# Second dense layer of the last MLP as fp32r in two parts, last y made by ScalarE from z, buffers of the second graph layer dealt out as they fall free

## Chip, core and metric

The kernel runs on one core of one Trainium2 chip. The metric is the device time of one execution in microseconds (us). Tiles are given as partitions x elements. All data are fp32 in memory; the matmuls work either on fp32 directly or on fp32r, a rounded form of the same width.

## Reference

```python
# x, x2: 4096 x 128; adj: 4096 x 4096
def cxin_conv(x, a, eps, W, b):
    ax = a @ x
    h = ax + (1.0 + eps[0]) * ax
    for i in range(3):
        h = relu(h @ W[i].T + b[i])
    return h
out1, out2 = cxin_conv(x, adj, eps1, W1, b1), cxin_conv(x2, adj, eps2, W2, b2)
x = layernorm(x + concatenate((out1, out2), axis=1) @ Wm.T + bm)
A_hat = adj + eye(4096)
d = rsqrt(sum(A_hat, axis=1))
x = layernorm(x + ((d[:, None] * A_hat * d[None, :]) @ x) @ W.T + b)
```

## The kernel before, in words

Everything is kept transposed. The adjacency is read twice, in four quarters of 1024 rows (QW) each: once for graph layer 0 (products with x and x2), once for graph layer 1 (product with y, the normalised x times the degree factor d). A quarter has 32 tiles (JB) of 128 x 1024, loaded in pairs of 1 MB by SP (`load` L371). Each tile is split in two fp32r parts: ScalarE rounds it to a high part (`round_a` L652, the activation at L684), VectorE subtracts to get the low part (`split_a` L838, L851), and TensorE multiplies high by high, high by low and low by high (`products` L465, L506). So a tile costs 12 matmuls of 512 columns in layer 0 and 6 in layer 1. The parts live in rings: four slots in layer 0 (SPLIT), six in layer 1 (SPLIT2); slots 4 and 5 of layer 1 are the tile hhi (high) and alo_extra (low), chosen by `ring_hi` L310 and `ring_lo` L318. A slot may be overwritten when TensorE has finished the tile six (in layer 0, four) back (`used_ahead` L323).

Pairs of layer 0 sit in four places (raw). Layer 1 has eight: raw and raw2; raw2 lies over x2 in memory and its parts fall free one after the other in quarter 3 of layer 0 (`load2` L381). Pair p of layer 1 goes to place p mod 8, first raw 0 to 3, then raw2 0 to 3 (`raw_tile` L266).

The order on each engine is written by hand: every engine runs the same loop over the tiles n of a quarter and does, at steps given by constants (L69 to L103), the extra work of the quarter before. That work (plan 0 for quarters 0 to 2, plan 1 for the last one, which falls in quarter 0 of layer 1) is: ScalarE evacuates the products to h (L698), three dense layers (`dense` L512) each followed by a ReLU (`relu` L701), the merge with Wm (`merge` L528), then the residual and statistics on VectorE (`residual` L884, `statistics` L923, `aggregate` L933), the power on GpSimd (`norm_power` L1156), `shifts` L945, and ScalarE's `normalise` L710, which writes xn. VectorE turns and sums the row sums (`turn_rowsums` L890, `add_turned` L895), SP carries them through memory (L386, L391), VectorE makes the degrees and the factors d (`degrees` L902, `degree_factors` L916). In plan 0 the dense layers are three fp32r passes over hhi and hlo, in plan 1 one fp32 matmul; there they stand behind tiles 1, 2 and 3, the merge behind tile 4.

```python
                    if plan == 0:
                        wait(pe, hlo_ready, q * (LAYERS * M) + (M * l + m + 1))
                        passes = ((whi, hhi), (whi, hlo), (wlo, hhi))
                    else:
                        wait(pe, h_ready, q * (4 * M) + (M * l + m + 1))
                        passes = ((par, h),)
```

y of a quarter is made in three steps: `make_y` L985 (VectorE, xn times d to yt), `round_y` L735 (ScalarE), `split_y` L996 (VectorE). The y of the last quarter is needed by TensorE at tile 24 of quarter 0 of layer 1 (L618). Before a tile of the diagonal is rounded, VectorE adds the identity to its square of 128 (`add_identity` L1015); in quarter 0 of layer 1 these are tiles 0 to 7, each added three steps ahead (AHEAD), so that three fall in the last steps of layer 0 and five in layer 1.

Of the kernel before, what the change touches and what calls it, by code (L numbers as in the profile page):

```python
# [67 lines left out]

PE_DENSE = ({3: 0, 5: 1, 8: 2}, {1: 0, 2: 1, 3: 2})  # L69
PE_MERGE = (10, 4)  # L70
PE_PROJECT = 1
# [4 lines left out]
ACT_EVACUATE = (2, 2)  # L76
ACT_RELU = tuple({k + ahead: l for k, l in plan.items()} for plan, ahead in zip(PE_DENSE, AHEAD_OF_PE))
DVE_RESIDUAL = tuple(k + ahead for k, ahead in zip(PE_MERGE, AHEAD_OF_PE))
STATISTICS = (2, KB)
TB = 32  # L80
GROUPS = P // TB
DVE_AGGREGATE = (DVE_RESIDUAL[0] + 1 + KB // STATISTICS[0], DVE_RESIDUAL[1])
DVE_DEGREES = tuple(k + 1 + plan for plan, k in enumerate(DVE_RESIDUAL))
DVE_FACTORS = (DVE_AGGREGATE[0] + 2, DVE_DEGREES[1] + 3)
DVE_TURN = (5, 4)
DVE_BASE = 10
DVE_BASE_LAST = 20
DVE_SHIFT = tuple(k + 2 for k in DVE_AGGREGATE)
ACT_NORM = (22, 14)
ACT_COPY_AY = 3  # L90
DVE_MAKE_Y = (KB + 4, 2 * KB + 4, 3 * KB + 3, 18)
NORM_BLOCKS = (2, 2)
# [20 lines left out]
SECOND_TILE = [(b, c, k) for c in range(CH) for b in range(2) for k in (0, 2)]  # L113
SECOND_TILE += [(b, c, 1) for c in range(CH) for b in range(2)]
X_AFTER = {1: 1, 3: 2, 6: 3, 12: 4, 20: 5}


def build(nc, a_t, head, early, x12, params, scratch, out):
    with ExitStack() as ctx:
# [22 lines left out]
        xn = sb("xn", [P, QUARTERS, QW])  # L142
        raw = sb("raw", [P, RAW, 2, QW])
        ahi = sb("ahi", [P, SPLIT, QW], F32R)
        alo = sb("alo", [P, SPLIT, QW], F32R)
        h = sb("h", [P, M, CW])
        hhi = sb("hhi", [P, M, CW], F32R)
        rowsum_all = sb("rowsum_all", [P, QW])
        xb = sb("xb", [P, KB, P])
# [23 lines left out]
        degpow = sb("degpow", [P, KB])  # L173
        dall = sb("dall", [P, QUARTERS, KB])

        ps = [ctx.enter_context(nc.psum_tensor(f"ps{i}", [P, CW], F32)) for i in range(M)]
# [49 lines left out]
        d_ready = sem("d_ready")  # L226
        yt_ready = sem("yt_ready")
        yhi_ready = sem("yhi_ready")
        base_ready = sem("base_ready")
# [36 lines left out]
        def raw_tile(layer, n):  # L266

            p = n // 2
            if layer == 0:
                return raw[:, p % RAW, n % 2, :]  # L270
            p %= RAW + RAW2
            return raw[:, p, n % 2, :] if p < RAW else raw2[:, p - RAW, n % 2, :]

        def wait_raw1(eng, q, n):

            s, turn = n // 2 % (RAW + RAW2), n // 2 // (RAW + RAW2)
# [33 lines left out]
        def ring_hi(layer, q, n):  # L310

            i = slot(layer, q, n)
            if i >= SPLIT:
                m = 2 * (i - SPLIT)
                return hhi[:, m:m + 2, :].rearrange("p m w -> p (m w)")
            return ahi[:, i, :]

# [28 lines left out]
        def _(sp):  # L346
# [34 lines left out]
            def load2(g):  # L381

                sp.wait_ge(block_used, (QUARTERS - 1) * JB + (g + 1) * KB)
                load(raw2[:, g], RAW + g).then_inc(raw2_in[g], 16)

# [39 lines left out]
            for s in range(RAW):  # L425
                sp.wait_ge(raw_used, groups * RAW + s + 1 - RAW)
                load(raw[:, s], s).then_inc(raw_in[s], 16)
                if s == 0:
                    load2(2)
            load2(3)  # L430
            turns = groups * RAW // (RAW + RAW2)

            def load1(g, s):

                sp.wait_ge(lo_ready, g * (2 * (RAW + RAW2)) + (QUARTERS * JB + 2 * (s + 1 - RAW - RAW2)))
                dst, landed = (raw[:, s], raw_in[s]) if s < RAW else (raw2[:, s - RAW], raw2_in[s - RAW])
                load(dst, g * (RAW + RAW2) + s).then_inc(landed, 16)

            for s in range(RAW + RAW2):
                load1(1, s)  # L440
                if s == 2:
                    spread_partial(LAST)
                if s == 3:
                    gather_partial(LAST)
            with sp.Fori(2, turns - turns // QUARTERS) as g:
                for s in range(RAW + RAW2):
                    load1(g, s)
            for m in range(PAIRS):

                s, c = m % (RAW + RAW2), m // (PAIRS // CH)  # L450
# [3 lines left out]
                for r, done in enumerate((unit_in[s], landed)):  # L454
                    sp.dma_start(dst[:, r, :].rearrange("p (t w) -> p t w", w=CW),
                                 a_t[pair + r][:, :, c * CW:(c + 1) * CW]).then_inc(done, 16)
# [7 lines left out]
        def _(pe):  # L464
# [179 lines left out]
        def _(act):  # L644
# [7 lines left out]
            def round_a(q, layer, n):  # L652
# [19 lines left out]
                else:  # L672
# [28 lines left out]
            def relu(q, l, plan):  # L701
                for m in range(M):
# [16 lines left out]
            def mlp_step(q, n, plan):  # L719
# [7 lines left out]
                at, size = ACT_NORM[plan], NORM_BLOCKS[plan]  # L727
                if at <= n < at + KB // size:
# [98 lines left out]
        def _(dve):  # L827
# [39 lines left out]

            def split_h(q, l, m):

                wait(dve, hhi_ready, q * (LAYERS * M) + (M * l + m + 1))  # L870
                dve.tensor_tensor(hlo[:, m, :], h[:, m, :], as_f32(hhi[:, m, :]),  # L871
                                  ALU.subtract).then_inc(hlo_ready, 1)
# [78 lines left out]
            def mlp_step(q, n, plan):  # L951
                if plan == 0:
                    if n in (ACT_EVACUATE[0] + 1, ACT_EVACUATE[0] + 2):
                        for m in range(CH):
                            split_h(q, 0, CH * (n - ACT_EVACUATE[0] - 1) + m)
                    if n in ACT_RELU[0] and ACT_RELU[0][n] < LAYERS - 1:
                        for m in range(M):
                            split_h(q, ACT_RELU[0][n] + 1, m)
                if n == DVE_TURN[plan]:
                    turn_rowsums(q)  # L960
                if n == DVE_TURN[plan] + 1:
                    add_turned(q)
# [94 lines left out]
            def layer0_quarter(q, before):  # L1057
                for n in range(JB):
# [8 lines left out]
                    if q is QUARTERS - 1:  # L1067
# [82 lines left out]
        def _(pool):  # L1150
# [22 lines left out]
            with pool.Fori(0, QUARTERS - 1) as q:  # L1173
                degree_power(q)
                norm_power(q + 1)
            norm_power(QUARTERS)
            degree_power(QUARTERS - 1)
            for q in range(QUARTERS - 1):
# [46 lines left out]
```

## Time and profile before

| | before |
|---|---|
| times of three runs | 593.35, 595.50, 595.93 us, median 595.5 |
| the profiled execution | 593.42 us, span 591.6 |
| granted TensorE clock in the profile | 1.000 |
| TensorE busy | 584.4 us, 99% |
| VectorE busy | 542.0 us, 92% |
| ScalarE busy | 372.3 us, 63% |
| GpSimd busy | 28.2 us, 5% |
| read from memory | 139.40 MB; moved in all 239 GB/s over the span |

The span runs from the first to the last instruction of the profiled execution. Layer 0 ends and layer 1 begins at about 390 us. A matmul's recorded duration overlaps with the next one's, so TensorE's prices are read from distances of starts.

### The profile page before, as it was taken

The numbers are of one execution on the slowest core, as the hardware profiler recorded it, in microseconds if no ns is written. First come the engines' busy times: TensorE is split into PE (matmuls) and PEld (weight loads), VectorE is DVE, ScalarE is ACT, GpSimd is POOL, SyncE is SP. The second block draws the span as 40 slices with busy tenths as digits, with TensorE's granted clock in tenths as the row PEclk, the third lists the DMA queues.
The fourth block names the chain that finished last, engine by engine and source line by source line (L and its number), as shares of the span: only waits on it lengthen the run. The fifth ranks groups of instructions, "written<-read, shape, count | busy, mean of one in ns | idle before, by whom it ended". The sixth has DMA issues, their size and how long they took to land.

```text
span 591.6 us, 7626 instructions
## 1 busy us (share of the span) xinstructions
PE 584.4 (99%) x2668; PEld 484.2 (82%) x2668; DVE 542.0 (92%) x683; ACT 372.3 (63%) x494; POOL 28.2 (5%) x26
## 2 busy tenths in 40 slices
PE   8999999999999999999999999999999999999996
PEld 7888888888888888888888888867888888888885
DVE  6999999998988998898799999995999999989986
ACT  6544447852454773454667336476897888898893
POOL 0000000001100000110000020000300010010011
PEclk9999999999999999999999999999999999999999
DMA  8968565444554543355444374785789999999911
GB/s 328 369 275 294 204 223 204 144 147 143 205 199 170 192 163 143 142 204 182 181 146 147 140 282 183 286 316 213 277 304 418 400 350 396 374 369 364 389 53 72
DMA packets 30730, 141.90 MB, mean 240 GB/s; under 512 B 5488, under 2 KB 6256, under 8 KB 16496
## 3 DMA queue, kind: packets, MB, share of 16 engines
q1 hardware_dynamic: 30128, 139.87, 63.6%
q10 hardware_dynamic: 576, 1.70, 0.7%
q8 instruction: 14, 0.23, 0.1%
q14 instruction: 12, 0.10, 0.0%
HBM read 139.40 MB, written 2.16 MB: 239 GB/s over the span
## 4 chain that ended last, share of the span: by engine, by line
PE 88%; DVE 10%; issue 1%; ACT 1%; POOL 0%; POOLq 0%; DVEq 0%; ACTq 0%
PE ps L506 71%; PE ps L579 7%; PE pd L524 5%; DVE alo L851 4%; PE pd L533 2%; DVE rowsum L866 2%; DVE rowsum L862 1%; PE pd L565 1%; PE pd L627 1%; ACT ahi L684 1%; DVE yt L994 0%; DVE x1lo L999 0%; DVE stats L928 0%; DVE raw L1020 0%; DVE outn L893 0%
## 5 line engine op out<-in xcount | busy, mean ns | idle before, releaser
L684 ACT ACTIVATE ahi<-raw 128x1024 fp32r<-128x1024 f32 x212 | 221.9, 1057 | 163.6 <-PE ps L506 149.1
L851 DVE TENSOR_TENSOR alo<-raw,ahi 128x1024 fp32r<-128x1024 f32 x212 | 258.1, 1224 | 28.9 <-ACT ahi L684 27.0
L506 PE MATMUL ps<-ahi,x2s 128*128 128x512 f32 x512 | 138.4, 389 | 0.0
L506 PE MATMUL ps<-ahi,x1hi 128*128 128x512 f32 x384 | 122.4, 394 | 0.1
L506 PE MATMUL ps<-ahi,x1lo 128*128 128x512 f32 x384 | 120.9, 391 | 0.0
L506 PE MATMUL ps<-alo,x1hi 128*128 128x512 f32 x384 | 120.5, 389 | 0.0
L506 PEld LDWEIGHTS ps<-ahi,x2s 128*128 128x128 f32 x512 | 96.2, 188 | 20.0
L506 PEld LDWEIGHTS ps<-ahi,x1hi 128*128 128x128 f32 x384 | 72.1, 189 | 16.1 <-issue 1.8
L506 PEld LDWEIGHTS ps<-ahi,x1lo 128*128 128x128 f32 x384 | 72.4, 189 | 14.9
L506 PEld LDWEIGHTS ps<-alo,x1hi 128*128 128x128 f32 x384 | 72.2, 188 | 15.0
L506 PE MATMUL ps<-alo,x2s 128*128 128x512 f32 x256 | 80.3, 389 | 0.0
L862 DVE TENSOR_TENSOR rowsum<-rowsum,raw 128x1024 f32<-128x1024 f32 x60 | 73.5, 1225 | 0.0
L866 DVE TENSOR_TENSOR rowsum<-rowsum,raw 128x1024 f32<-128x1024 f32 x56 | 68.6, 1224 | 0.0
L851 DVE TENSOR_TENSOR alo_extra<-raw,hhi 128x1024 fp32r<-128x1024 f32 x42 | 50.8, 1222 | 7.4 <-ACT hhi L684 6.9
L506 PEld LDWEIGHTS ps<-alo,x2s 128*128 128x128 f32 x256 | 48.1, 188 | 10.0
L684 ACT ACTIVATE hhi<-raw 128x1024 fp32r<-128x1024 f32 x42 | 43.5, 1053 | 9.1 <-PE ps L506 7.9
L1159 POOL TENSOR_TENSOR rstd<-vareps,halves 128x8 f32<-128x8 f32 (+2 forms) x10 | 19.4, 1935 | 249.3 <-DVE vareps L1050 143.5
L705 ACT ACTIVATE h<-pd,par 128x512 f32<-128x512 f32 x48 | 30.9, 679 | 0.4 <-PE pd L524 0.3
L871 DVE TENSOR_TENSOR hlo<-h,hhi 128x512 fp32r<-128x512 f32 x36 | 22.8, 696 | 0.0
L689 ACT ACTIVATE hhi<-h 128x512 fp32r<-128x512 f32 x36 | 22.1, 629 | 0.8
L1154 POOL TENSOR_TENSOR degpow<-degc,halves 128x8 f32<-128x8 f32 x4 | 7.5, 1886 | 310.2 <-DVE degpos L914 310.2
L506 PE MATMUL ps<-hhi,x1hi 128*128 128x512 f32 x64 | 20.6, 399 | 0.0
(95 smaller groups left out, 508.8 us busy)
## 6 DMA issues: line engine op xcount, KB each, us to landing
raw<-a_t SPq DMA_DIRECT2D x108, 1024.0 KB, 4.9
raw<-a_t SPq DMA_DIRECT2D x32, 512.0 KB, 7.8
raw<-early SPq DMA_DIRECT2D x7, 512.0 KB, 7.8
xn<-x SPq DMA_DIRECT2D x3, 1024.0 KB, 8.5
out<-outn ACTq DMA_DIRECT2D x3, 512.0 KB, 6.2
par<-params SPq DMA_DIRECT2D x1, 708.0 KB, 13.2
raw<-head SPq DMA_DIRECT2D x2, 256.0 KB, 3.5
xn<-x SPq DMA_DIRECT2D x1, 512.0 KB, 7.1
```

Source lines behind the costliest of these rows:

```text
L506: mm = pe.matmul(ps[bank + (CH * (q % 2) if layer else 0)][:, :], block_of(w, n), a[c], start=(n == 0 and k == 0), stop=(n == JB - 1 and k ...
L524: mm = pe.matmul(pd[:, m, :], w[:, at:at + P], a[:, m, :], start=(k == 0), stop=(k == len(passes) - 1))
L533: mm = pe.matmul(merged[:, k, :], h[:, CH * b + k // 4, (k % 4) * P:(k % 4 + 1) * P], par[:, WM_AT + b * P:WM_AT + (b + 1) * P], start=(k ...
L579: mm = pe.matmul(bank, block_of(w, j + t), a[:, at], start=(n == opens and t == 0 and k == 0), stop=(n == closes and t == 1 and k == 2), s ...
L684: act.activation(ring_hi(layer, q, n), raw_tile(layer, n), ACT.Copy).then_inc(hi_ready, 1)
L689: act.activation(hhi[:, m, :], h[:, m, :], ACT.Copy).then_inc(hhi_ready, 1)
L705: act.activation(h[:, m, :], pd[:, m, :], ACT.Relu, bias=par[:, at:at + 1]).then_inc(h_ready, 1)
L851: dve.tensor_tensor(ring_lo(layer, q, n), raw_tile(layer, n), as_f32(ring_hi(layer, q, n)), ALU.subtract).then_inc(lo_ready, 1)
L862: dve.tensor_tensor(rowsum[:, :], rowsum[:, :], tile, ALU.add).then_inc(rowsum_step, 1)
L866: dve.tensor_tensor(to[:, :], rowsum[:, :], tile, ALU.add).then_inc(raw_used, 1)
L871: dve.tensor_tensor(hlo[:, m, :], h[:, m, :], as_f32(hhi[:, m, :]), ALU.subtract).then_inc(hlo_ready, 1)
L1159: pool.tensor_tensor(rstd[:, r], vareps[:, r], halves[:, r], ALU.pow).then_inc(rstd_ready, 1)
```

## The change

The dense layers of plan 1 move to tiles 1, 3 and 5 and the merge to tile 6, with ScalarE's ReLUs at its tiles 4, 6 and 7 (before 7, 8 and 9). The second of them is done in fp32r in three passes: ScalarE writes ReLU 0 twice, as h and rounded as hhi, and VectorE subtracts in place (h_rest lies over h). hhi is no longer a ring slot; two new tiles take its place (ahi_extra), one of which lies over rowsum_all, so that the high part of tile 5 waits for the transpose of the row sums. The transpose and its sum move to VectorE's step 2. ScalarE makes the last y from z itself, with scale rstd x d and bias shift x d, at its steps 13 to 16; VectorE's product for it goes; the normalisation of that quarter to xn moves to ScalarE's steps 22 to 29. The order of the eight places of layer 1 changes: pairs 0 and 1 go to raw2, whose first parts are free earliest. All eight identities of quarter 0 are added in the last eight steps of layer 0. SP's two steps for the degrees each move ahead of two loads. GpSimd does the last degree power before the norm power.

```diff
-PE_DENSE = ({3: 0, 5: 1, 8: 2}, {1: 0, 2: 1, 3: 2})
-PE_MERGE = (10, 4)
+PE_DENSE = ({3: 0, 5: 1, 8: 2}, {1: 0, 3: 1, 5: 2})
+PE_MERGE = (10, 6)
+DVE_SPLIT_H = {4: 1}
...
-ACT_RELU = tuple({k + ahead: l for k, l in plan.items()} for plan, ahead in zip(PE_DENSE, AHEAD_OF_PE))
-DVE_RESIDUAL = tuple(k + ahead for k, ahead in zip(PE_MERGE, AHEAD_OF_PE))
+ACT_RELU = ({k + SPLIT: l for k, l in PE_DENSE[0].items()}, {4: 0, 6: 1, 7: 2})
+DVE_RESIDUAL = (PE_MERGE[0] + SPLIT, PE_MERGE[1] + SPLIT)
...
-DVE_DEGREES = tuple(k + 1 + plan for plan, k in enumerate(DVE_RESIDUAL))
+DVE_DEGREES = (DVE_RESIDUAL[0] + 1, DVE_RESIDUAL[1] - 1)
...
-DVE_TURN = (5, 4)
+ACT_NORM_LAST = 22
+DVE_TURN = (5, 2)
...
-ACT_NORM = (22, 14)
+ACT_NORM = (22, 13)
...
-DVE_MAKE_Y = (KB + 4, 2 * KB + 4, 3 * KB + 3, 18)
+DVE_MAKE_Y = (KB + 4, 2 * KB + 4, 3 * KB + 3, 16)
...
+SLOT1 = (4, 5, 0, 1, 6, 2, 3, 7)
...
-            p %= RAW + RAW2
+            p = SLOT1[p % (RAW + RAW2)]
...
-            if i >= SPLIT:
-                m = 2 * (i - SPLIT)
-                return hhi[:, m:m + 2, :].rearrange("p m w -> p (m w)")
-            return ahi[:, i, :]
+            return ahi[:, i, :] if i < SPLIT else ahi_extra[SPLIT2 - 1 - i][:, :]
...
-            for s in range(RAW + RAW2):
-                load1(1, s)
-                if s == 2:
+            for i in range(RAW + RAW2):
+                load1(1, i)
+                if i == 0:
                     spread_partial(LAST)
-                if s == 3:
+                if i == 1:
                     gather_partial(LAST)
...
+                    elif l == 1:
+                        wait(pe, hlo_ready, q * (LAYERS * M) + (M * (l - 1) + m + 1))
+                        passes = ((whi, hhi), (whi, h_rest), (wlo, hhi))
...
+                if layer == 1 and q == 0 and n == SPLIT2 - 1:
+                    act.wait_ge(turned_ready, QUARTERS)
...
+                    if plan == 1 and l == 0:
+                        act.activation(hhi[:, m, :], pd[:, m, :], ACT.Relu,
+                                       bias=par[:, at:at + 1]).then_inc(hhi_ready, 1)
...
+            def last_y(blocks):
+
+                if blocks[0] == 0:
+                    act.wait_ge(y_scales_ready, 2)
+                    act.wait_ge(y_ready, LAST)
+                for k in blocks:
+                    i = act.activation(yt[:, k, :], z[:, k, :], ACT.Identity,
+                                       scale=y_scale[:, k:k + 1], bias=y_shift[:, k:k + 1])
+                if k == KB - 1:
+                    i.then_inc(yt_ready, 1)
...
+                        if ACT_NORM_LAST <= n < ACT_NORM_LAST + KB:
+                            normalise(QUARTERS, lambda k: xn[:, LAST, k * P:(k + 1) * P], xn_ready, (n - ACT_NORM_LAST,))
...
+                if n == DVE_FACTORS[plan]:
+                    degree_factors(q)
                 if n == DVE_SHIFT[plan]:
                     shifts(q + 1)
-                if n == DVE_FACTORS[plan]:
-                    degree_factors(q)
+                    if plan == 1:
+                        dve.wait_ge(d_ready, QUARTERS)
+                        dve.wait_ge(norm_ready, QUARTERS)
+                        dve.tensor_tensor(y_scale[:, :], rstd[:, :], dall[:, LAST, :], ALU.mult).then_inc(y_scales_ready, 1)
+                        dve.tensor_tensor(y_shift[:, :], nshift[:, :], dall[:, LAST, :], ALU.mult).then_inc(y_scales_ready, 1)
...
-                    if n == DVE_MAKE_Y[g]:
+                    if g < LAST and n == DVE_MAKE_Y[g]:
                         make_y(g)
...
-                        if n + AHEAD >= JB:
-                            add_identity(0, n + AHEAD - JB)
+                        if n >= JB - KB:
+                            add_identity(0, n + KB - JB)
...
-                        if n + AHEAD < KB:
-                            add_identity(q, n + AHEAD)
+                        if n in DVE_SPLIT_H:
+                            for m in range(M):
+                                split_h(LAST, DVE_SPLIT_H[n], m, 1)
...
-            norm_power(QUARTERS)
             degree_power(QUARTERS - 1)
+            norm_power(QUARTERS)
```

## Rows read from the trace of the kernel before

**Rows 1.** The page, busy time and the chain by engine.

```profile
PE 584.4 (99%) x2668; PEld 484.2 (82%) x2668; DVE 542.0 (92%) x683; ACT 372.3 (63%) x494; POOL 28.2 (5%) x26
...
PE 88%; DVE 10%; issue 1%; ACT 1%; POOL 0%; POOLq 0%; DVEq 0%; ACTq 0%
```

**Rows 2.** The chain of waits in order of time: start us, us, what.

```profile
321.13 2.72 PE pd L524 x12
...
402.72 3.43 PE pd L524 x8
...
407.53 3.57 PE pd L533 x32
...
411.10 39.46 PE ps L506 x174
```

**Rows 3.** The timeline of TensorE: start us, us, engine, line, operation.

```profile
392.56 3.60 PE L524 MATMUL pd<-h,par 128*128 128x512 f32 x8
...
395.59 1.03 PE L506 MATMUL ps<-ahi,x1hi 128*128 128x512 f32 x2
...
396.91 0.61 PE L506 MATMUL ps<-alo,x1hi 128*128 128x512 f32 x2
...
400.77 1.03 PE L506 MATMUL ps<-ahi,x1hi 128*128 128x512 f32 x2
```

**Rows 4.** Windows: us, busy PE PEld DVE ACT POOL, clock, DMA share, GB/s.

```profile
372.00:382.00 10.00, 10.00 (x46) 8.29 (x45) 10.00 (x10) 4.03 (x5) 0.00 (x0) 1.00 0.81 315
...
415.00:425.00 10.00, 10.00 (x45) 8.26 (x44) 9.12 (x14) 8.80 (x14) 5.16 (x2) 1.00 0.72 274
```

**Rows 5.** The timeline at the end of layer 0, VectorE and TensorE's weight load.

```profile
382.36 0.29 DVE L1020 TENSOR_TENSOR raw<-raw,identity 128x128 f32<-128x128 f32 x1
...
382.56 1.23 DVE L851 TENSOR_TENSOR alo<-raw,ahi 128x1024 fp32r<-128x1024 f32 x1
...
385.03 1.23 DVE L851 TENSOR_TENSOR alo<-raw,ahi 128x1024 fp32r<-128x1024 f32 x1
...
387.35 0.19 PEld L506 LDWEIGHTS ps<-alo,x1hi 128*128 128x128 f32 x1
```

**Rows 6.** The timeline of ScalarE, ReLUs and normalisation.

```profile
396.92 2.40 ACT L705 ACTIVATE h<-pd,par 128x512 f32<-128x512 f32 x4
...
406.19 0.69 ACT L705 ACTIVATE h<-pd,par 128x512 f32<-128x512 f32 x1 [0.17 <-PE pd L524]
...
418.32 0.88 ACT L714 ACTIVATE xn<-z,nshift,rstd 128x128 f32<-128x128 f32 x2 [0.61 <-DVE nshift L948]
...
419.11 1.05 ACT L684 ACTIVATE ahi<-raw 128x1024 fp32r<-128x1024 f32 x1
...
420.05 0.87 ACT L714 ACTIVATE xn<-z,nshift,rstd 128x128 f32<-128x128 f32 x2
```

**Rows 7.** The page's groups by line, the old rounding of h.

```profile
L689 ACT ACTIVATE hhi<-h 128x512 fp32r<-128x512 f32 x36 | 22.1, 629 | 0.8
```

**Rows 8.** The timeline of VectorE: split of h, residual, tile, degrees, shift.

```profile
308.96 2.51 DVE L871 TENSOR_TENSOR hlo<-h,hhi 128x512 fp32r<-128x512 f32 x4
...
411.14 1.23 DVE L888 TENSOR_TENSOR z<-pd,xb 128x1024 f32<-128x1024 f32 x1 [1.20 <-PE pd L533]
...
414.83 1.22 DVE L851 TENSOR_TENSOR alo_extra<-raw,hhi 128x1024 fp32r<-128x1024 f32 x1
...
417.11 0.38 DVE L905 TENSOR_REDUCE together<-regrouped 128x32 f32<-128x128 f32 x1
...
418.12 0.16 DVE L948 SCALAR_TENSOR_TENSOR nshift<-mv,rstd 128x8 f32<-128x8 f32 x1
```

**Rows 9.** The timeline of GpSimd, its two powers.

```profile
340.21 1.64 POOL L1154 TENSOR_TENSOR degpow<-degc,halves 128x8 f32<-128x8 f32 x1 [84.61 <-DVE degpos L914]
...
415.00 2.54 POOL L1159 TENSOR_TENSOR rstd<-vareps,halves 128x8 f32<-128x8 f32 x1 [60.74 <-DVE vareps L943]
```

**Rows 10.** The loads of the adjacency at L374, issue to landing.

```profile
DMA to landing us min/median/max: 4.6/4.9/12.6
```

More of the change, by code:

```diff
@@ L143, in build @@
         raw = sb("raw", [P, RAW, 2, QW])
+        with ExitStack() as until_turned:
+            rowsum_all = until_turned.enter_context(nc.sbuf_tensor("rowsum_all", [P, QW], F32))
+        ahi_extra = [sb(f"ahi_extra{i}", [P, QW], F32R) for i in range(SPLIT2 - SPLIT)]
+        with ExitStack() as whole:
+            h = whole.enter_context(nc.sbuf_tensor("h", [P, M, CW], F32))
+        h_rest = sb("h_rest", [P, M, CW], F32R)
         ahi = sb("ahi", [P, SPLIT, QW], F32R)
         alo = sb("alo", [P, SPLIT, QW], F32R)
-        h = sb("h", [P, M, CW])
         hhi = sb("hhi", [P, M, CW], F32R)
-        rowsum_all = sb("rowsum_all", [P, QW])
         xb = sb("xb", [P, KB, P])
@@ L174, in build @@
         dall = sb("dall", [P, QUARTERS, KB])
+        y_scale = sb("y_scale", [P, KB])
+        y_shift = sb("y_shift", [P, KB])
         ps = [ctx.enter_context(nc.psum_tensor(f"ps{i}", [P, CW], F32)) for i in range(M)]
@@ L227, in build @@
         yt_ready = sem("yt_ready")
+        y_scales_ready = sem("y_scales_ready")
         yhi_ready = sem("yhi_ready")
@@ L270, in raw_tile @@
                 return raw[:, p % RAW, n % 2, :]
-            p %= RAW + RAW2
+            p = SLOT1[p % (RAW + RAW2)]
             return raw[:, p, n % 2, :] if p < RAW else raw2[:, p - RAW, n % 2, :]
         def wait_raw1(eng, q, n):
-            s, turn = n // 2 % (RAW + RAW2), n // 2 // (RAW + RAW2)
+            s, turn = SLOT1[n // 2 % (RAW + RAW2)], n // 2 // (RAW + RAW2)
             per_quarter = 16 * PAIRS // (RAW + RAW2)
@@ L383, in load2 @@
                 sp.wait_ge(block_used, (QUARTERS - 1) * JB + (g + 1) * KB)
-                load(raw2[:, g], RAW + g).then_inc(raw2_in[g], 16)
+                load(raw2[:, g], SLOT1.index(RAW + g)).then_inc(raw2_in[g], 16)
             def spread_partial(q):
@@ L426, in _ @@
                 sp.wait_ge(raw_used, groups * RAW + s + 1 - RAW)
-                load(raw[:, s], s).then_inc(raw_in[s], 16)
-                if s == 0:
+                load(raw[:, s], SLOT1.index(s)).then_inc(raw_in[s], 16)
+                if s == 1:
                     load2(2)
@@ L431, in _, with load1 @@
             turns = groups * RAW // (RAW + RAW2)
-            def load1(g, s):
-                sp.wait_ge(lo_ready, g * (2 * (RAW + RAW2)) + (QUARTERS * JB + 2 * (s + 1 - RAW - RAW2)))
+            def load1(g, i):
+                s = SLOT1[i]
+                sp.wait_ge(lo_ready, g * (2 * (RAW + RAW2)) + (QUARTERS * JB + 2 * (i + 1 - RAW - RAW2)))
                 dst, landed = (raw[:, s], raw_in[s]) if s < RAW else (raw2[:, s - RAW], raw2_in[s - RAW])
-                load(dst, g * (RAW + RAW2) + s).then_inc(landed, 16)
-            for s in range(RAW + RAW2):
-                load1(1, s)
-                if s == 2:
+                load(dst, g * (RAW + RAW2) + i).then_inc(landed, 16)
+            for i in range(RAW + RAW2):
+                load1(1, i)
+                if i == 0:
                     spread_partial(LAST)
-                if s == 3:
+                if i == 1:
                     gather_partial(LAST)
             with sp.Fori(2, turns - turns // QUARTERS) as g:
-                for s in range(RAW + RAW2):
-                    load1(g, s)
+                for i in range(RAW + RAW2):
+                    load1(g, i)
             for m in range(PAIRS):
-                s, c = m % (RAW + RAW2), m // (PAIRS // CH)
+                i, c = m % (RAW + RAW2), m // (PAIRS // CH)
+                s = SLOT1[i]
                 pair = LAST * PAIRS + 2 * QUADS[c][m % (PAIRS // CH)]
@@ L453, in _ @@
                 dst, landed = (raw[:, s], raw_in[s]) if s < RAW else (raw2[:, s - RAW], raw2_in[s - RAW])
-                for r, done in enumerate((unit_in[s], landed)):
+                for r, done in enumerate((unit_in[i], landed)):
                     sp.dma_start(dst[:, r, :].rearrange("p (t w) -> p t w", w=CW),
@@ L727, in mlp_step @@
                 at, size = ACT_NORM[plan], NORM_BLOCKS[plan]
-                if at <= n < at + KB // size:
+                if plan == 1:
+                    if at <= n < at + KB // size:
+                        last_y(range(size * (n - at), size * (n - at + 1)))
+                elif at <= n < at + KB // size:
                     if isinstance(q, int):
@@ L866, in sum_rows, with split_h @@
                     dve.tensor_tensor(to[:, :], rowsum[:, :], tile, ALU.add).then_inc(raw_used, 1)
-            def split_h(q, l, m):
-                wait(dve, hhi_ready, q * (LAYERS * M) + (M * l + m + 1))
-                dve.tensor_tensor(hlo[:, m, :], h[:, m, :], as_f32(hhi[:, m, :]),
+            def split_h(q, l, m, plan):
+                if plan == 1:
+                    wait(dve, h_ready, q * (4 * M) + (M * l + m + 1))
+                wait(dve, hhi_ready, q * (LAYERS * M) + (M * (l - plan) + m + 1))
+                dve.tensor_tensor((hlo, h_rest)[plan][:, m, :], h[:, m, :], as_f32(hhi[:, m, :]),
                                   ALU.subtract).then_inc(hlo_ready, 1)
@@ L954, in mlp_step @@
                         for m in range(CH):
[L955 to L958, printed above, removed]
+                            split_h(q, 0, CH * (n - ACT_EVACUATE[0] - 1) + m, 0)
+                if plan == 0 and n in ACT_RELU[0] and ACT_RELU[0][n] < LAYERS - 1:
+                    for m in range(M):
+                        split_h(q, ACT_RELU[0][n] + 1, m, 0)
                 if n == DVE_TURN[plan]:
                     turn_rowsums(q)
-                if n == DVE_TURN[plan] + 1:
+                if n == DVE_TURN[plan] + 1 - plan:
                     add_turned(q)
@@ L1090, in layer1_quarter @@
                     elif q == 0:
-                        if n + AHEAD < KB:
-                            add_identity(q, n + AHEAD)
+                        if n in DVE_SPLIT_H:
+                            for m in range(M):
+                                split_h(LAST, DVE_SPLIT_H[n], m, 1)
                     elif (n + AHEAD2) // KB == q:
@@ L1175, in _ @@
                 norm_power(q + 1)
+            degree_power(QUARTERS - 1)
             norm_power(QUARTERS)
-            degree_power(QUARTERS - 1)
             for q in range(QUARTERS - 1):
```

1 line of the change is left out of this document (added).

## The prediction

> **What bounds the kernel now.** I read the page's busy shares and its chain by engine and line first. TensorE is busy 99% of the span and 88% of the chain is its own work; the 10% of VectorE in the chain says that it runs close behind [rows 1]. The chain in order of time then gives TensorE's prices [rows 2]: 174 product matmuls of 512 columns in 39.46 us are 0.227 us each, so a tile of layer 1 (6 matmuls) takes 1.36 us; a dense layer of four matmuls as plain fp32 takes 3.43 us, 0.857 each; the same four in fp32r, as three passes, take 2.72 us in the earlier quarters; the merge takes 3.57 us. One dense layer of the last MLP holds TensorE longer. Dense 0 starts at 392.56 and the next tile at 395.59, 3.03 later; dense 1 could start two matmul slots after 396.91, at 397.36, and the next tile starts at 400.77, 3.41 later [rows 3]. The 0.38 us are a stop: the first ReLU 0 left ScalarE only at 397.6 (396.92 + 0.69, [rows 6]). So the most that this change can take from TensorE's path is 0.71 + 0.38 = 1.09 us. The start and the tail are not touched.
>
> Next the windows [rows 4]: VectorE is 10.00 of 10 us busy late in layer 0 and 9.12 of 10 in the layer-1 window in which the last statistics and y are made, ScalarE 8.80 of 10 there. These two have to stay ahead of TensorE, and they are what the change loads differently.
>
> **TensorE.** Dense 0 starts at 392.56 [rows 3] as before. Then in the new order: 3.43 to 395.99, two tiles to 398.71, dense 1 in three passes 2.72 to 401.43, two tiles to 404.16, dense 2 3.43 to 407.58, one tile to 408.94, merge 3.57 to 412.51, where tile 7 begins. Before, tile 5 begins at about 410.95 (0.15 under the chain's 411.10 [rows 2], where the overlap of pipelined matmuls is counted) and tile 7 at 413.67: 1.16 us later, my 1.09 within rounding. The dense saving, 0.71, is the difference of two measured rows. The Trainium skill (FP8 and Floating Point Precision, TensorE Precision Notes) counts a true FP32 matmul as four passes; by that four matmuls cost 3.63 us and the saving is 0.91, an estimate. The row says 3.8 passes, and I keep 0.71.
>
> **Is dense 1 fed in time?** ScalarE now does ReLU 0 after tile 4 and writes it twice, to h and to hhi: eight instructions at the 0.57 us pitch of four in 2.40 [rows 6], from 393.6 to 398.1. The second copy is not in the trace; its bounds are 0.57 and the 0.63 us of the old rounding from h [rows 7]. VectorE subtracts four times, 0.60 us each (2.51 for four, [rows 8]), behind the low part of tile 4. Those subtracts run from about 396.6 to 399.1; TensorE wants the first at 398.7 and the last at 400.75. No wait. Moving the transpose and the reduce (1.13 us each) ahead of tile 3 costs nothing here either: low part 3 is done at 395.5, TensorE wants it at 398.3. SP's two DMA steps for the degrees move ahead of loads that are not yet released; the degrees are read more than 10 us after, so they cost nothing.
>
> **The identities.** Eight instead of three now stand inside quarter 3 of layer 0, each displacing VectorE by 0.20 us (382.36 to 382.56, [rows 5]). There VectorE has no idle time, so low part 31 ends 1.0 us later: from 386.26 (385.03 + 1.23) to 387.26. TensorE loads the weights for it at 387.35 [rows 5]. It just fits; bounds 0 and 0.2 us, taken 0. The first tile of layer 1 has about 0.3 more. The same five leave layer 1. They need pairs 2 and 3 of the adjacency, whose places fall free after steps 25 and 27 and which are wanted after steps 28 and 30. Between lie three VectorE steps of 2.27 us (385.03 - 382.56 - 0.20, [rows 5]), one y product or split of 1.14 and 0.6 of identities: 8.5 us. The transfer lands in 4.9 [rows 10]. Covered.
>
> **The new wait, where I put the result.** Follow ScalarE from ReLU 2. It follows dense 2 and ends at 408.3 (it ended 406.9 before, [rows 6]). Roundings 8, 9 and 10 stand behind it (0.95 each). The low parts of 8 and 9 run on VectorE from 409.4, then the degrees (1.0 us: 417.11 to the shift's 418.12, [rows 8]), then low part 10, then the residual at 413.8. The merge was done at 412.8, so it is not what is late; VectorE's own order is. Before, VectorE stood waiting for the merge and began at 411.14. Residual, statistics, aggregate and variance take 3.7 us (411.14 to low part 11 at 414.83, [rows 8]): to 417.5. POOL's power then takes 2.54 [rows 9] to 420.2, the shift and the two new scale products 0.4, and they are ready at 420.7.
>
> ScalarE does step 13 (rounding 13) at 414.1 and next stands at the wait for these scales, 5.7 us, with roundings 14 and on queued behind. Before, its normalisation came one step later and it waited 0.6 [rows 6]. TensorE starts tile 14 at 412.51 + 7 x 1.361 = 422.0. ScalarE gives y blocks 0 and 1 (0.79 a pair, [rows 6]), rounding 14 at 421.5 to 422.5: already late. From there a step of ScalarE takes 0.79 + 0.95 = 1.74 against TensorE's 1.36, three times more, so the last y pair ends at 426.7, rounding 17 at 427.7, the rounding of y at 428.6, rounding 18 at 429.7. VectorE does low part 18, then the split of y (1.14), then low part 19, done at 433.2. TensorE wants low part 19 at 412.51 + 12 x 1.361 + 0.91 = 429.75. It restarts a weight load after its data (0.2: in the stop before dense 1 the data were late by 0.2 and the stop was 0.38), so the hold is 3.64 us. Behind it nothing repeats: eight more normalisations of 0.40 ride with roundings of 0.95, 1.35 against 1.36, so ScalarE keeps pace without gaining, and later quarters start again with full rings.
>
> What the change removes from VectorE, one y product, and the shorter way through one engine less are in this timetable already: they bring y forward but do not help, since the ring of six tiles is emptied by ScalarE's wait. The end of layer 1 is TensorE-bound and takes the hold over whole.
>
> **Sum:** -0.71 - 0.38 + 3.64 = +2.55 us. It stands on an execution of 593.42 us (span 591.6 and 1.8 around it), which is 2.1 below the median of 595.5; the four times shown lie in two pairs, at 593.4 and 595.5 to 595.9. I take their mean, 594.6, and get 597.2 us. Bounds of the hold: 2.7 if POOL takes the 1.64 us of its other power [rows 9], 4.3 with 0.3 us of lag after the merge, 0.2 at tile 31 and 0.2 in the chain. Net +1.6 to +3.2.
>
> A rule speaks about the y blocks. The trace shows 0.79 us of ScalarE per pair of 128-column blocks [rows 6]. The Trainium skill (Perfetto Trace Analysis, Optimizing Scalar/DVE Operations) puts ScalarE's overhead at about 93 ns per instruction on SBUF and advises grouping work where the engine is saturated; with 128 columns at the pace of the 1024-column row a pair would take 0.40, an estimate, and the sum would be +1.0.
>
> **Rivals.**
> 1. ScalarE's wait does no harm: the scales come before 417 because VectorE reaches the residual with the merge, or more lead survives than I count. Then only TensorE's gain is left, -1.1: 593.5 us. For it: VectorE stood idle for 1.20 us before the merge ended [rows 8], and every margin ahead of the scales is positive. Against: residual at 413.8 by three queues in order. 0.22.
> 2. Slower, by the loads: VectorE now waits inside saturated quarter 3 for pairs 2 and 3. The place is the identity of tile 4, after step 28. It decides once the transfer takes over 8.5 us; at the 12.6 seen as maximum [rows 10] VectorE stands for 4.1 us, tile 31 has 0.1 of margin and TensorE loses 4.0 more: 601.2 us. Against: that maximum needs a crowded queue, and these windows move data with ease [rows 4]. 0.06.
> 3. The y pairs cost only by their columns: 256 of the 1024 for which a rounding takes 0.95, so 0.24 us. A step of ScalarE is then 1.19, no longer slower than TensorE's, and the hold shrinks by four times 0.55 to 1.4. Net +0.3: 594.9 us. Against it, the normalisation has the same shape, and its row says 0.79 [rows 6]. 0.04. The overhead rule above stands between the two.
> 4. The dense layer in parts saves nothing, if its three passes interrupt for their operands: +3.2 with the hold. It lies in my case's upper bound, and the 2.72 us three times over speak against it.
>
> **How the numbers follow.** About 0.5%, 3.0 us, is what a measurement of this kernel can tell from no change. My case has 0.60; it straddles that line, 0.38 within and 0.22 slower. Rival 1 is within (0.20, and 0.02 faster by the scatter of the runs), rival 2 slower, rival 3 within. The last 0.08 is for what I do not see: 0.03 faster, 0.02 within, 0.03 slower. That is 0.05, 0.64 and 0.31. The range goes from rival 1 (593.5) to my upper bound on the slower pair of runs (595.7 + 3.2, with scatter 599.9); my own case alone spans 595.0 to 599.5.
>
> **What would show it.** Dense 1 as 12 matmuls in 2.72 us with no stop before it; ScalarE with one wait of 5 to 6 us for the new scale products, at about 415 to 421; VectorE's residual near 413.8 without waiting for the merge; TensorE with short stops from about 421 to 433 summing to 3 to 4 us, and none in tile 31. If TensorE runs without stops from 412.5 on, I am wrong and rival 1 holds. If it stops at tile 31 or at the first tiles of layer 1, the identities cost more than I said.

## The result, and the profile after

The changed kernel takes 595.98 us (median of 21 runs, 595.46 to 598.38) against 593.31 us before (median of 21 runs, 592.81 to 595.93): 2.67 us more, a ratio of 1.0045 with a 95% interval of 1.0037 to 1.0052. That is slower, and within the half per cent, if narrowly: the interval's upper end lies just above it. The profiled execution took 595.72 us with a span of 593.7.

Busy time and its shares hardly move. In the page's chain by engine TensorE's share falls from 88% [rows 1] to 84% and ScalarE, 1% before, has 4%, but this is no measure of the loss: the same line of the later runs has TensorE at 72% in a4_single, which is faster than the changed kernel, and at 93% in a3_fp32, which is slower.

```profile
PE 585.4 (99%) x2672; PEld 483.4 (81%) x2672; DVE 543.8 (92%) x688; ACT 376.3 (63%) x506; POOL 29.2 (5%) x26
...
PE 84%; DVE 7%; ACT 4%; issue 2%; POOL 1%; DMA 1%; SPq 0%; POOLq 0%; DVEq 0%; ACTq 0%
```

**The stretch.** The start of the kernel differs by up to 2.3 us between the profiled executions (last section), so I compare the traces from the first matmul of dense 0 to the start of the third projection, when layer 1 is in its last quarter. Here are its two ends in the timeline of TensorE (start us, us, engine, line, operation), first the one row of before that is not among the rows above:

```profile
541.03 1.95 PE L565 MATMUL pd<-par,h 128*128 128x128 f32 x16
```

```profile
392.09 3.59 PE L536 MATMUL pd<-h,par 128*128 128x512 f32 x8
...
543.13 1.95 PE L577 MATMUL pd<-par,h 128*128 128x128 f32 x16
```

Before it is 541.03 - 392.56 [rows 3] = 148.47 us, after 543.13 - 392.09 = 151.04: 2.57 more. The whole difference of the medians lies in it, and the forecast sum was 2.55.

**TensorE's part** in the timeline after: the second dense layer, the tile behind it, the merge and the second pair of matmuls of tile 7. The last row is the first pair of tile 7 before.

```profile
398.25 0.39 PE L536 MATMUL pd<-hhi,whi 128*128 128x512 f32 x1
...
400.97 0.62 PE L515 MATMUL ps<-ahi_extra,x1hi 128*128 128x512 f32 x2
...
408.50 3.73 PE L545 MATMUL pd<-par,h 128*128 128x128 f32 x32
...
412.54 0.62 PE L515 MATMUL ps<-ahi,x1lo 128*128 128x512 f32 x2
```

```profile
413.67 0.61 PE L506 MATMUL ps<-ahi,x1hi 128*128 128x512 f32 x2
```

Twelve matmuls in 2.72 us (400.97 - 398.25), with no stop before them. Tile 7 begins two slots of 0.227 ahead of its second pair at 412.54, that is at 412.09, 20.0 us after dense 0; before it began 21.1 after it (413.67 - 392.56). The gain of 1.1 us is there. From tile 7 to the third projection it is 543.13 - 412.09 = 131.04 us, before 541.03 - 413.67 = 127.36. This loss of 3.68 us is the hold, the sum of TensorE's stops, which the prediction put at 3.64.

**The hold**, in the timeline of ScalarE (in brackets what it waited for and how long):

```profile
413.65 1.06 ACT L698 ACTIVATE ahi<-raw 128x1024 fp32r<-128x1024 f32 x1 [0.90 <-PE ps L515]
...
420.40 0.88 ACT L761 ACTIVATE yt<-z,y_shift,y_scale 128x128 f32<-128x128 f32 x2 [5.69 <-DVE y_shift L1023]
...
422.14 0.86 ACT L761 ACTIVATE yt<-z,y_shift,y_scale 128x128 f32<-128x128 f32 x2
```

Rounding 13 at 413.65, then 5.69 us at the wait for the scale products, then steps of 422.14 - 420.40 = 1.74 us. Before, ScalarE waited 0.61 us at that place [rows 6]. The timeline of VectorE shows why the scales come late:

```profile
411.27 0.38 DVE L940 TENSOR_REDUCE together<-regrouped 128x32 f32<-128x128 f32 x1
...
412.28 1.22 DVE L884 TENSOR_TENSOR alo_extra<-raw,ahi_extra 128x1024 fp32r<-128x1024 f32 x1
...
413.42 1.22 DVE L923 TENSOR_TENSOR z<-pd,xb 128x1024 f32<-128x1024 f32 x1
...
420.20 0.16 DVE L1023 TENSOR_TENSOR y_shift<-nshift,dall 128x8 f32<-128x8 f32 x1
...
431.60 3.49 DVE L884 TENSOR_TENSOR alo<-raw,ahi 128x1024 fp32r<-128x1024 f32 x3
```

The degrees (411.27), low part 10 (412.28) and the residual (413.42) follow each other without a wait; before, the residual stood with 1.20 us of idle time ahead of it [rows 8]. Counted from dense 0 the residual comes 2.75 us later than before (21.33 against 411.14 - 392.56 = 18.58). Two things make this up: the merge itself ends 1.6 us later (412.23 - 392.09 = 20.14, before 411.10 - 392.56 = 18.54 [rows 2]), and VectorE takes the residual up 1.19 us after the merge's end, where it took it up at once. The row at 431.60 begins with low part 19. TensorE's own stops are small, in its timeline:

```profile
421.56 0.73 PE L515 MATMUL ps<-alo,x1hi 128*128 128x512 f32 x2 [0.17 <-DVE alo L884]
...
432.87 0.73 PE L515 MATMUL ps<-alo,x1hi 128*128 128x512 f32 x2 [0.61 <-DVE alo L884]
```

and in the waits of the window 380 to 440 us (engine, line, what it waited for: us in total, times, longest), its weight loads:

```profile
PEld ps L515 <- DVE alo L884: 3.1, 5, 1.0
...
PEld ps L515 <- DVE alo_extra L884: 1.1, 3, 0.5
...
PEld ps L515 <- ACT ahi L698: 0.9, 3, 0.4
...
PEld ps L515 <- ACT ahi_extra L698: 0.2, 1, 0.2
```

Eight waits for low parts and four for high parts, none over 1.0 us. (The idle time of the weight loads is more than the time lost, as they run ahead of the matmuls.) The time is lost in thin slices, which the busy shares do not show: TensorE is at 99% in both kernels.

### The profile page after: what moved, and what is told of

Its sections match the earlier page's. It is cut to its first block, busy times and chain, and to the rows that moved or that the text cites. A ratio compares the mean times of both kernels' runs of the same rounds, so it can differ in the third digit from the quotient of the medians.

```text
span 593.7 us, 7657 instructions
## 1 busy us (share of the span) xinstructions
PE 585.4 (99%) x2672; PEld 483.4 (81%) x2672; DVE 543.8 (92%) x688; ACT 376.3 (63%) x506; POOL 29.2 (5%) x26
## 4 chain that ended last, share of the span: by engine, by line
PE 84%; DVE 7%; ACT 4%; issue 2%; POOL 1%; DMA 1%; SPq 0%; POOLq 0%; DVEq 0%; ACTq 0%
PE ps L515 74%; PE pd L536 6%; DVE alo L884 3%; PE pd L545 2%; ACT ahi L698 2%; PE ps L591 1%; POOL rstd L1200 1%; PE pd L577 1%; DMA raw<-early 1%; ACT ahi_extra L698 1%; ACT outn L788 1%; DVE rowsum L895 1%; ACT outn L731 0%; ACT yt L761 0%; DVE alo_extra L884 0%
## 5 line engine op out<-in xcount | busy, mean ns | idle before, releaser
L884 DVE TENSOR_TENSOR alo_extra<-raw,ahi_extra 128x1024 fp32r<-128x1024 f32 x42 | 50.8, 1221 | 4.5 <-ACT ahi_extra L698 4.1
L698 ACT ACTIVATE ahi_extra<-raw 128x1024 fp32r<-128x1024 f32 x42 | 43.6, 1054 | 4.3 <-PE ps L515 2.8
L515 PE MATMUL ps<-alo_extra,x1hi 128*128 128x512 f32 x64 | 20.3, 394 | 0.1
```

Source lines behind the costliest of these rows:

```text
L515: mm = pe.matmul(ps[bank + (CH * (q % 2) if layer else 0)][:, :], block_of(w, n), a[c], start=(n == 0 and k == 0), stop=(n == JB - 1 and k ...
L884: dve.tensor_tensor(ring_lo(layer, q, n), raw_tile(layer, n), as_f32(ring_hi(layer, q, n)), ALU.subtract).then_inc(lo_ready, 1)
```

## The experiments

Eight kernels were run, each timed against the kernel before in five rounds. The stretch is read as above. In the expectations I called its end "the end of the third projection" and quoted 148.64 and 151.21: these are the chain's figures for that projection's start, 0.17 above the timeline's. Differences are the same in both. In the table's expected column, a1 to a4 and the changed kernel have the difference of times against before, b1 to c1 that of the stretch.

| kernel | stretch us | against before | expected | median us (before 593.66) | ratio, 95% interval |
|---|---|---|---|---|---|
| changed | 151.04 | +2.57 | +2.55 | 595.98 (593.31) | 1.0045, 1.0037 to 1.0052 |
| a1_y_late | 147.90 | -0.57 | -0.6 | 593.53 | 0.9999, 0.9990 to 1.0008 |
| a2_y14 | 149.69 | +1.22 | +1.2 | 595.17 | 1.0025, 1.0013 to 1.0037 |
| a3_fp32 | 151.77 | +3.30 | +3.3 | 597.30 | 1.0062, 1.0048 to 1.0075 |
| a4_single | 149.40 | +0.93 | +0.9 | 594.95 | 1.0024, 1.0014 to 1.0034 |
| b1_late_shift | 147.42 | -1.05 | -1.0 | 592.78 | 0.9985, 0.9976 to 0.9995 |
| b3_ids_back | 147.92 | -0.55 | -0.5 | 593.23 | 0.9992, 0.9983 to 1.0001 |
| b4_old_y | 150.53 | +2.06 | +2.1 | 595.75 | 1.0034, 1.0022 to 1.0046 |
| c1_third_dense | 147.12 | -1.35 | -1.5 | 592.09 | 0.9975, 0.9966 to 0.9985 |

### a1_y_late: the last y at later steps

```diff
-ACT_NORM = (22, 13)
+ACT_NORM = (22, 16)
-DVE_MAKE_Y = (KB + 4, 2 * KB + 4, 3 * KB + 3, 16)
+DVE_MAKE_Y = (KB + 4, 2 * KB + 4, 3 * KB + 3, 19)
```

> The changed kernel with only the steps of the last y moved: ScalarE makes it at its steps 16 to 19 instead of 13 to 16, rounds it at 20, VectorE splits it at 21 instead of 18. Main theory (ScalarE's wait for the scales with roundings 14 to 18 queued behind it is the loss): TensorE's stops from tile 14 on vanish, only 0.4 us before low part 13 stay; against the kernel before -0.6 us, ratio 0.999; against the changed kernel -3.2 us. ScalarE's idle time before its first y activation falls from 5.7 us to under 1. Rival (the loss comes from what was added to VectorE and moved ahead: identities, subtractions, degrees before the residual): the time stays 2.7 us above the kernel before, ratio 1.0045.

TensorE's ends of the stretch, and two waits of the window 380 to 450 us:

```profile
394.39 3.59 PE L536 MATMUL pd<-h,par 128*128 128x512 f32 x8
...
542.29 1.95 PE L577 MATMUL pd<-par,h 128*128 128x128 f32 x16
```

```profile
ACT yt L761 <- DVE y_shift L1023: 1.5, 1, 1.5
...
PEld ps L515 <- DVE alo L884: 0.6, 1, 0.6
```

Two numbers were changed and 3.14 us of stretch are gone. ScalarE still waits for the scales, for 1.5 us instead of 5.7 (I had said under 1), but now with roundings up to 16 done, and of the weight loads' waits two are left, 0.6 us before low part 13 and 0.2 before low part 11. The rival, that the work added to VectorE is the loss, falls. The median is only 0.1 below the kernel before where 0.6 were expected; the interval holds both, and the profiled execution, the slowest of the eleven, reached dense 0 at 394.39, 2.3 us later than that of the changed kernel. The saving is read from the stretch; the medians alone do not show it.

### a2_y14: one step later

```diff
-ACT_NORM = (22, 13)
+ACT_NORM = (22, 14)
-DVE_MAKE_Y = (KB + 4, 2 * KB + 4, 3 * KB + 3, 16)
+DVE_MAKE_Y = (KB + 4, 2 * KB + 4, 3 * KB + 3, 17)
```

> The changed kernel with the last y one step later only (ScalarE steps 14 to 17, rounding at 18, split at 19). Main theory: one more rounding stands ahead of the wait, so the hold shrinks by one TensorE tile, 1.36 us: +1.2 us against the kernel before, ratio 1.002. Rival (loss elsewhere): +2.7 us, ratio 1.0045.

```profile
392.99 3.59 PE L536 MATMUL pd<-h,par 128*128 128x512 f32 x8
...
542.68 1.95 PE L577 MATMUL pd<-par,h 128*128 128x128 f32 x16
```

```profile
ACT yt L761 <- DVE y_shift L1023: 4.3, 1, 4.3
```

The stretch is 1.35 us shorter than in the changed kernel: one tile of TensorE (1.36), for one rounding that stands ahead of the wait and not behind it. ScalarE's wait shrinks by 1.4.

### a3_fp32: the second dense layer as fp32 again

```diff
-                    elif l == 1:
-                        wait(pe, hlo_ready, q * (LAYERS * M) + (M * (l - 1) + m + 1))
-                        passes = ((whi, hhi), (whi, h_rest), (wlo, hhi))
...
-                    if plan == 1 and l == 0:
-                        act.activation(hhi[:, m, :], pd[:, m, :], ACT.Relu,
-                                       bias=par[:, at:at + 1]).then_inc(hhi_ready, 1)
...
-                        if n in DVE_SPLIT_H:
-                            for m in range(M):
-                                split_h(LAST, DVE_SPLIT_H[n], m, 1)
+                        pass
```

> The changed kernel with its second dense layer as plain fp32 again: no second write of ReLU 0, no subtraction, one fp32 matmul per output. All steps stay. Main theory: TensorE has 0.71 us more before the merge, and the hold behind it is unchanged, since ScalarE and VectorE follow the third dense layer: +3.3 us against the kernel before, ratio 1.0055. Rival (the added subtractions and second ReLU are what makes ScalarE and VectorE late): the time falls below the changed kernel's, +1.5 us or less, ratio 1.0025 or less.

```profile
394.40 3.60 PE L533 MATMUL pd<-h,par 128*128 128x512 f32 x8
...
546.17 1.95 PE L574 MATMUL pd<-par,h 128*128 128x128 f32 x16
```

0.73 us longer than the changed kernel. So the dense layer in parts saves what the two rows of before say (3.43 against 2.72 [rows 2]), and the second ReLU and the subtractions do not feed the hold. By the medians, each against its own runs of before, the difference is 1.0 us (3.64 against 2.67), with intervals that overlap.

### a4_single: y in single blocks

```diff
-NORM_BLOCKS = (2, 2)
+NORM_BLOCKS = (2, 1)
-DVE_MAKE_Y = (KB + 4, 2 * KB + 4, 3 * KB + 3, 16)
+DVE_MAKE_Y = (KB + 4, 2 * KB + 4, 3 * KB + 3, 20)
```

> The changed kernel with the last y made in single blocks at eight steps (13 to 20), rounding at 21, split at 22. The wait for the scales stays where it was, only the pace of ScalarE's steps behind it changes: 0.40 + 0.95 = 1.35 us instead of 1.74. Main theory (late start and slow pace add up): the first stop of 0.3 to 0.5 us stays, the growth of 0.38 us per step goes, about 2.0 us of stops in place of 3.7: +0.9 us against the kernel before, ratio 1.0015. Rival (the 5.7 us wait alone sets the loss, whatever follows): +2.6 us, ratio 1.0045.

```profile
392.82 3.59 PE L536 MATMUL pd<-h,par 128*128 128x512 f32 x8
...
542.22 1.95 PE L577 MATMUL pd<-par,h 128*128 128x128 f32 x16
```

```profile
ACT yt L761 <- DVE y_shift L1023: 5.7, 1, 5.7
```

The wait is the same 5.7 us and yet 1.64 of the 3.68 us of hold are gone. So the wait spends the lead, and ScalarE's pace behind it, 1.74 us a step against TensorE's 1.36, adds nearly half of the hold. Of the 2.04 us left, 0.89 stand before low part 23, which VectorE now makes behind its split of y; in the changed kernel 0.90 stand before low part 19, in the same place behind the split.

### b1_late_shift: the shift behind low part 13 as well

```diff
-ACT_NORM = (22, 13)
+ACT_NORM = (22, 17)
-DVE_MAKE_Y = (KB + 4, 2 * KB + 4, 3 * KB + 3, 16)
+DVE_MAKE_Y = (KB + 4, 2 * KB + 4, 3 * KB + 3, 20)
-DVE_SHIFT = tuple(k + 2 for k in DVE_AGGREGATE)
+DVE_SHIFT = (DVE_AGGREGATE[0] + 2, DVE_AGGREGATE[1] + 3)
```

> The changed kernel with the last y at ScalarE's steps 17 to 20, rounding at 21, split at 22, and VectorE's shift and scales one step later, behind low part 13 instead of before it. Main theory: the stop before low part 13 (0.6 us idle of TensorE's weight load in a1_y_late) goes too, TensorE runs without stops from dense 0 on but for one under 0.1 us before low part 11. The stretch from TensorE's dense 0 to the end of its third projection, 148.64 us before and 151.21 in the changed kernel, is 147.6 to 147.7. Time against the kernel before -1.0 us, ratio 0.998, against a1_y_late -0.4. Rival (the stop moves to a later tile, since ScalarE is full): the stretch stays at 148.1, as in a1_y_late.

```profile
392.23 3.59 PE L536 MATMUL pd<-h,par 128*128 128x512 f32 x8
...
539.65 1.95 PE L577 MATMUL pd<-par,h 128*128 128x128 f32 x16
```

```profile
PEld ps L515 <- DVE alo_extra L884: 0.2, 1, 0.2
```

The only wait of a weight load for an engine in the window 385 to 450 us is 0.2 us, before low part 11. The stretch is 1.05 us shorter than before: nearly all of TensorE's gain of 1.1 is kept. The stop did not move to a later tile, as the rival had it.

### b3_ids_back: a1_y_late with the identities where they were

```diff
-                        if n >= JB - KB:
-                            add_identity(0, n + KB - JB)
+                        if n + AHEAD >= JB:
+                            add_identity(0, n + AHEAD - JB)
...
                                 split_h(LAST, DVE_SPLIT_H[n], m, 1)
+                        if n + AHEAD < KB:
+                            add_identity(q, n + AHEAD)
```

> a1_y_late with the eight identities where the kernel before has them: three in the last steps of layer 0, five in layer 1, each three steps ahead. Main theory (the moved identities cost and bring nothing, tile 31 had just margin enough): stretch dense 0 to third projection 148.1 us as in a1_y_late, time within 0.3 us of it; low part 31 ends about 1.1 us before TensorE loads its weights instead of 0.1 to 0.3. Rival (moving them saves time in layer 1): 0.5 to 1.0 us slower than a1_y_late.

The ends of the stretch, and low part 31 with the weight load that needs it, here and in the changed kernel:

```profile
392.97 3.59 PE L536 MATMUL pd<-h,par 128*128 128x512 f32 x8
...
540.89 1.95 PE L577 MATMUL pd<-par,h 128*128 128x128 f32 x16
...
385.45 1.21 DVE L884 TENSOR_TENSOR alo<-raw,ahi 128x1024 fp32r<-128x1024 f32 x1
...
387.76 0.19 PEld L515 LDWEIGHTS ps<-alo,x1hi 128*128 128x128 f32 x1
```

```profile
385.58 1.21 DVE L884 TENSOR_TENSOR alo<-raw,ahi 128x1024 fp32r<-128x1024 f32 x1
...
386.88 0.19 PEld L515 LDWEIGHTS ps<-alo,x1hi 128*128 128x128 f32 x1
```

With the identities moved, low part 31 is ready 0.09 us before its weight load (386.88 - 386.79), with the old places 1.10 (387.76 - 386.66). The stretch, which holds the five identities of layer 1, is the same to 0.02 us. For the part in layer 0, which lies ahead of the stretch, the chains of waits give the time from the merge of quarter 2 to dense 0: 63.27 us here and in the changed kernel. The move cost nothing and brought nothing.

### b4_old_y: the old way to the last y

```diff
-ACT_NORM = (22, 13)
+ACT_NORM = (22, 14)
-DVE_MAKE_Y = (KB + 4, 2 * KB + 4, 3 * KB + 3, 16)
+DVE_MAKE_Y = (KB + 4, 2 * KB + 4, 3 * KB + 3, 18)
...
-                if plan == 1:
-                    if at <= n < at + KB // size:
-                        last_y(range(size * (n - at), size * (n - at + 1)))
-                elif at <= n < at + KB // size:
+                if at <= n < at + KB // size:
...
-                        dve.tensor_tensor(y_scale[:, :], rstd[:, :], dall[:, LAST, :], ALU.mult).then_inc(y_scales_ready, 1)
-                        dve.tensor_tensor(y_shift[:, :], nshift[:, :], dall[:, LAST, :], ALU.mult).then_inc(y_scales_ready, 1)
...
-                    if g < LAST and n == DVE_MAKE_Y[g]:
+                    if n == DVE_MAKE_Y[g]:
```

> The changed kernel with the old way to the last y at the old steps: ScalarE normalises to xn at steps 14 to 17, VectorE makes y at 18, ScalarE rounds it at 19, VectorE splits it at 20; no scale products. All else as changed. Main theory: the wait for the residual is late by the same 2.7 us and the old way has one engine more in it: ScalarE waits about 4 us at its step 14, then stops follow up to tile 21, 3.2 us in all, +2.1 us against the kernel before (stretch 150.8), ratio 1.0035. So not ScalarE's making of y by itself but the place of that wait behind a late residual is the loss. Rival (the new way to y is the loss): the time falls to the kernel before or below, stretch 148.0 or less.

```profile
393.05 3.60 PE L536 MATMUL pd<-h,par 128*128 128x512 f32 x8
...
543.58 1.95 PE L577 MATMUL pd<-par,h 128*128 128x128 f32 x16
```

```profile
ACT xn L731 <- DVE nshift L978: 3.9, 1, 3.9
```

The same two steps of normalising and multiplying as before, at the same step numbers, now leave the kernel 2.06 us slower than before, because ScalarE waits 3.9 us where it waited 0.61 [rows 6]. The new way to y is not the loss: it is the wait behind a late residual. That the residual is late is read from the traces; no run moved it or the degrees ahead of it.

### c1_third_dense: the third dense layer in fp32r too

```diff
-                    elif l == 1:
+                    elif l >= 1:
...
-                    if plan == 1 and l == 0:
+                    if plan == 1 and l < LAYERS - 1:
...
-DVE_SPLIT_H = {4: 1}
+DVE_SPLIT_H = {4: 1, 6: 2}
```

beside the edits of b1_late_shift.

> b1_late_shift with the third dense layer of the last MLP in fp32r as well: ReLU 1 written twice, four more subtractions on VectorE behind low part 6. Main theory: TensorE saves another 0.71 us, of which 0.2 come back as a stop of 0.3 before low part 11, since residual and statistics stand ahead of it on VectorE: stretch 147.1 us, time against the kernel before -1.5 us, ratio 0.9975. Rival (ScalarE's four more writes hold up rounding 7 and ReLU 2): stretch 147.7 or more, no gain over b1_late_shift.

```profile
392.29 3.59 PE L536 MATMUL pd<-h,par 128*128 128x512 f32 x8
...
539.41 1.95 PE L577 MATMUL pd<-par,h 128*128 128x128 f32 x16
```

```profile
PEld ps L515 <- DVE alo_extra L884: 0.5, 1, 0.5
...
PEld pd L545 <- ACT h L719: 0.2, 1, 0.2
```

This version beats both kernels: 592.09 us, 0.25% below the kernel before and 0.7% below the changed one (0.9975 divided by 1.0045 is 0.993). Of the 0.71 us of the third dense layer 0.30 are kept, less than the 0.5 expected. The stop before low part 11 was foreseen, at 0.3 us, and is where the rest went: up to the second pair of tile 7 the saving is 0.69 us (19.76 from dense 0 against 20.45 in b1_late_shift), and 0.36 of it are lost between tiles 11 and 12. The wait of the merge's weight load for the last ReLU 2 (0.2 us) was not foreseen and costs next to nothing. The medians of the two kernels differ by 0.69 us, and their intervals overlap.

## Why the prediction was right, point by point

The forecast was 597.2 us, no change within half a per cent, +2.55 us; measured are 595.98 us, +2.67 by the medians and +2.57 in the stretch. The steps of the forecast came out nearly as written, with two exceptions named below. The execution of after reached dense 0 at 392.09 instead of 392.56, so its times stand 0.47 us below the forecast's.

- **Dense 1 and its stop, -1.09:** the trace has -1.1, and a3_fp32 shows the 0.71 of it by itself (0.73). The rule of four passes in the Trainium skill (FP8 and Floating Point Precision, TensorE Precision Notes) would have made this 0.91; the rows were nearer.
- **Feeding dense 1, no wait:** none is in the trace, and the second copy of ReLU 0 took the lower of its two bounds, 0.57 us.
- **The identities, it just fits:** forecast 0.09 us of margin for low part 31, measured 0.09. b3_ids_back puts their effect at 0.02 us in the stretch and at nothing ahead of it.
- **The residual late by VectorE's own order:** forecast 413.8, measured 413.42 + 0.47 = 413.9. The order alone makes 1.19 of the 2.75 us; the rest is the merge, which stands two tiles further back. The forecast had both times and blamed only the order.
- **The scales at 420.7, ScalarE's wait of 5.7:** the last product ends at 420.36, with 0.47 that is 420.8; the wait is 5.69. POOL took the 2.54 of its row, so the lower bound of the hold was not needed.
- **Steps of 1.74 us, low part 19 done at 433.2:** measured 1.74, and 431.60 + 1.22 + 0.47 = 433.3. The hold was forecast as 3.64 us and is 3.68. The y blocks cost 0.79 us a pair, as the row of the normalisation said. The estimate from the Trainium skill (Perfetto Trace Analysis, Optimizing Scalar/DVE Operations), 0.40 a pair, is not borne out here, and with it rival 3 falls.
- **Rival 1, no harm,** falls with ScalarE's 5.7 us and with a1_y_late. **Rival 2, the loads,** falls too: VectorE has no wait on a load from 340 to 400 us, and tile 31 no stop. The 12.6 us that it rested on belong to the first load of [rows 10], issued at 10.8 us, when the DMA share was 1.04; from 340 to 390 us none took more than 7.0. **Rival 4** falls with a3_fp32.

**What was off** is the level, not the change. I took the mean of the two pairs of times, 594.6, as the place of the kernel before. With 21 runs it is 593.31; most runs lie near the profiled execution's 593.42, and the upper pair were the rarer ones. The forecast of 597.2 was 1.2 us too high for that reason alone. The profiled execution, for which the sum was made, was the better base. That the forecast still fell on the right side of its 3.0 us line owes something to luck: the sum lay 0.45 us under it, and the forecast gave slower 0.31. The range had flaws too: its end of 599.9 adds a scatter of 1.0 us and that of my own case, 599.5, one of 0.6, with no row behind either, and rival 2's 601.2 lies outside it.

One sentence of the forecast said the removed VectorE product brings y forward but does not help. The last part was wrong. With ScalarE's wait in the same place, behind rounding 14, the new way is 0.84 us cheaper than the old (a2_y14 +1.22, b4_old_y +2.06). It is the start one step earlier, 1.35 us dearer (a2_y14 against the changed kernel), that turns this into a loss of 0.5.

## What to carry to other kernels

In a kernel with hand-written orders a step that waits should not stand as early as its input might come (later steps were better here up to step 17, the latest that was tried): everything queued behind it on the same engine waits with it, and a ring's lead is spent without any sign in the busy shares. After a wait, compare the engine's step with that of the engine it feeds: here 1.74 us against 1.36 made 1.6 of the 3.7 us of hold (a4_single). A timetable by hand, walking the in-order queues with starts and distances from one trace, gave the change to 0.1 us; the busy shares, 99% for TensorE in both kernels, would have said that nothing happens.

## What the runs showed of the hardware

The same layer 0 took different times up to dense 0 of the last MLP: 392.09 us in the changed kernel, 392.23 in b1_late_shift, 394.39 and 394.40 in a1_y_late and a3_fp32 (one profiled execution each, and their code is the same up to there), 392.56 before. The chains of the first part of a1_y_late and of b1_late_shift begin with the first load of the adjacency:

```profile
1.66 4.57 DMA raw<-head
...
7.02 99.34 PE ps L515 x430
```

```profile
1.66 3.97 DMA raw<-head
...
6.43 97.77 PE ps L515 x430
```

0.6 us of the difference are the load's own landing, the other 1.6 lie inside the first 430 product matmuls of layer 0 (99.34 against 97.77). The timeline of TensorE shows where: the first of these matmuls and the ninth and tenth, of a1_y_late and then of b1_late_shift.

```profile
7.02 0.77 PE L515 MATMUL ps<-ahi,x1hi 128*128 128x512 f32 x1 [0.78 <-ACT ahi L675]
...
10.52 0.63 PE L515 MATMUL ps<-ahi,x2s 128*128 128x512 f32 x2
```

```profile
6.43 0.47 PE L515 MATMUL ps<-ahi,x1hi 128*128 128x512 f32 x1 [0.26 <-ACT ahi L675]
...
8.32 0.62 PE L515 MATMUL ps<-ahi,x2s 128*128 128x512 f32 x2
```

The first eight take 3.50 us in a1_y_late and 1.89 in b1_late_shift, and that is the 1.6. After the longer stop most of them follow each other every 0.43 us, which is 512 columns at 1.2 GHz, the lower level of TensorE's clock; after the shorter stop all but the first come every 0.23, the upper level. The profile's granted clock reads 1.00 in both stretches, so it shows nothing of this and the distances of starts do. a3_fp32, with a stop of 0.69 us at the same place, has 3.55 us for these eight. A first load that landed 0.6 us later thus goes with 2.2 us in these two traces. This also limits what the median of five or ten runs can tell here, and it is why the stretch was used.
